# A fused four-layer block on one NeuronCore: layernorms at three stage seams moved off GpSimd and worked by token groups, and maxima added by VectorE in the last softmax

## The reference

```python
x = x + _layernorm(attention(_layernorm(x)))     # 16 heads, band of 64 on either side
x = x + _layernorm(kmoe_ffn(_layernorm(x)))      # top 2 of 64 Kronecker experts
x = x + _layernorm(state_space(_layernorm(x)))
x = x + _layernorm(soft_moe(_layernorm(x)))

def state_space(x):                # inner width 256, state 64
    x_input, x_gate = split(x @ W_in.T)
    u = silu(causal_conv4(x_input) + conv_b)
    Bu = u @ W_B.T
    h_t = 0.95 * h_(t-1) + 0.05 * Bu_t                     # along the tokens
    y = (hs @ W_C.T + D_param * u) * silu(x_gate)
    y = y @ W_out.T
    return _layernorm(y + x) * ln_gamma + ln_beta

def soft_moe(x):                   # 64 experts, 32 slots each
    logits = (x @ phi_w.T + phi_b).reshape(tokens, 64, 32)
    D = softmax(logits, over the slots);  C = softmax(logits, over the experts)
    X = tanh(_layernorm(sums of x over all tokens, weighted by D))   # one row a slot
    return C @ (X @ expert_w + expert_b)
```

## Time and profile before

| | |
|---|---|
| device time, median of 3 runs | 782.77 us (781.86 to 792.21) |
| the profiled execution's own time | 791.13 us |
| its span | 789.4 us |
| TensorE busy | 656.1 us, 83% |
| VectorE busy | 475.5 us, 60% |
| ScalarE busy | 359.4 us, 46% |
| GpSimd busy | 340.2 us, 43% |
| mean granted clock of TensorE | 0.903 |

### The profile page before, as it was taken

One profiled execution on the slowest core, in us unless ns is written; L12 is line 12 of the kernel. 1 busy time (PEld: TensorE's weight loads), 2 busy tenths in 40 slices (PEclk: granted clock), 3 DMA queues, 4 the chain that ended last, 5 costly groups with the idle time before them and its releaser, 6 DMA issues. The chain is left out here.

```text
span 789.4 us, 17996 instructions
## 1 busy us (share of the span) xinstructions
PE 656.1 (83%) x7326; PEld 373.9 (47%) x7326; DVE 475.5 (60%) x1242; ACT 359.4 (46%) x633; POOL 340.2 (43%) x368
## 2 busy tenths in 40 slices
PE   3598989999869999798828860799989879999995
PEld 1314545555427988677724430333333344444442
DVE  6556757785263334261375869699999861424455
ACT  3604646666657335242337431655445454334410
POOL 3004646666520000000015351299989927856531
PEclk9956979999788999898778995799999989999999
DMA  4523240000036400000019000000000000000000
GB/s 87 95 68 47 56 61 10 4 4 4 2 138 199 99 12 4 3 2 4 5 35 360 14 1 0 0 0 1 1 0 0 1 1 1 0 1 13 1 13 27
DMA packets 18389, 27.17 MB, mean 34 GB/s; under 512 B 3699, under 2 KB 16948, under 8 KB 17284
## 3 DMA queue, kind: packets, MB, share of 16 engines
q1 hardware_dynamic: 17390, 25.82, 13.0%
q10 hardware_dynamic: 918, 0.21, 0.2%
HBM read 18.11 MB, written 1.05 MB: 24 GB/s over the span
## 5 line engine op out<-in xcount | busy, mean ns | idle before, releaser
L491 ACT ACTIVATE at_exp<-at_psum 128x512 f32<-128x512 f32 x136 | 78.2, 606 | 62.3 <-PE at_psum L608 59.8
L1592 POOL TENSOR_TENSOR all_phi_b<-all_phi_b,mo_work 128x512 f32<-128x512 f32 x56 | 71.0, 1268 | 44.5 <-ACT mo_work L1798 40.1
L838 POOL TENSOR_TENSOR all_x<-all_x,ff_x_blocks 128x512 f32<-128x512 f32 x3 | 3.9, 1286 | 170.4 <-ACT ff_x_blocks L1029 170.4
L1613 PE MATMUL all_psum<-all_phi,mo_xt 128*128 128x512 f32 x128 | 66.1, 643 | 7.3 <-ACT mo_work L1780 5.6
L306 POOL TENSOR_SCALAR_AFFINE_SELECT at_exp<-at_exp 128x512 f32<-128x512 f32 x68 | 43.1, 634 | 63.9 <-ACT at_exp L491 63.9
L1562 POOL TENSOR_TENSOR mo_work<-mo_work,mo_max 128x1024 f32<-128x1024 f32 x32 | 61.4, 1920 | 21.3 <-DVE mo_max L1854 21.3
L363 DVE TENSOR_REDUCE at_neg_max<-at_psum 128x2 f32<-128x512 f32 x68 | 47.0, 691 | 33.6 <-PE at_psum L595 33.5
L1646 PE MATMUL all_psum<-mo_xt,all_phi_centred 128*128 128x512 f32 x128 | 66.2, 598 | 0.0
L1798 ACT ACTIVATE mo_work<-all_psum 128x512 f32<-128x512 f32 x64 | 37.7, 601 | 61.8 <-PE all_psum L1646 61.8
L595 PE MATMUL at_psum<-at_k_stack,at_q_stack 49*128 49x256 bf16 x272 | 59.1, 306 | 6.2 <-DMA at_k_stack<-at_part_l 3.2
L1699 PE MATMUL all_psum<-mo_work,mo_y_slots 128*128 128x512 f32 x128 | 62.5, 595 | 1.8 <-DVE mo_work L1902 1.8
(11 more groups left out here) (346 smaller groups left out, 1329.6 us busy)
## 6 DMA issues: line engine op xcount, KB each, us to landing
all_expert_w<-in_expert_w SPq DMA_DIRECT2D x1, 4096.0 KB, 18.1
ff_b_up<-in_b_up SPq DMA_DIRECT2D x1, 2048.0 KB, 9.7
ff_a_up<-in_a_up SPq DMA_DIRECT2D x1, 2048.0 KB, 14.1
ff_w_down<-in_w_down SPq DMA_DIRECT2D x2, 1024.0 KB, 18.7
at_q_stack<-at_part_h SPq DMA_DIRECT2D x24, 64.0 KB
at_k_stack<-at_part_h SPq DMA_DIRECT2D x24, 64.0 KB
at_q_stack<-at_part_m SPq DMA_DIRECT2D x16, 64.0 KB
at_k_stack<-at_part_m SPq DMA_DIRECT2D x16, 64.0 KB
```

Source lines behind the costliest of these rows:

```text
L491: nc.scalar.activation(e[:, m // 2, 2 * (m % 2):2 * (m % 2) + 2, :, :].rearrange("p h j q -> p (h j q)"), psum[:, ST + n % 3, :], ACT.Exp, ...
L1592: nc.gpsimd.tensor_tensor(tot[:, ch % 2, :], first, ec[:, ch % 2, j, :], ALU.add).then_inc(added, 1)
L1613: last = nc.tensor.matmul(psum[:, 2 * hf + k, :], xt[:, P * z:P * z + P], phi_d[:, HALF * hf + W * k:HALF * hf + W * k + W], start=True, s ...
```

## The change

1. `Norm.variance` folds the division by 128 into the root (`scale=1/P` in the ScalarE instruction) and has one operation less.
2. At the end of `kmoe` GpSimd adds nothing any more. VectorE adds each group to `x` (`add_x`, 128x512 at once, group 3 in two halves) and at once takes statistics and factors of the next stage's layernorm for groups 0 to 2; VectorE and ScalarE scale two tiles of each. The nine loads of `ssm` are issued in `kmoe`, behind that stage's own.
3. `ssm` starts with the last four tiles only. TensorE transposes quarter 0, runs `project(0)`, transposes quarters 1 to 3, and runs `project(1)`. ScalarE copies quarters 0 and 1, then takes the root of the last group, then `take_x(0)`. `project` waits bank by bank.
4. The bias of `phi` enters PSUM as a second product with one row of 1/128 (`inv_row`), so GpSimd neither scales nor adds it. VectorE gates the last quarter (`gated(3)`).
5. At the end of `ssm` ScalarE scales all tiles of both norms in groups (0 to 11, 12 to 15), VectorE applies gamma and beta as 128x512 products and sums, adds to `x` and takes the statistics of `soft_moe`'s layernorm for tiles 0 to 11; ScalarE scales 8 of them, and TensorE, after 12 products whose result nothing reads, transposes the first quarter. `soft_moe` starts with the last four tiles and the logits.
6. In the combine the 40 blocks from n = 24 on get their maxima from VectorE: the maxima of chunks 1 to 3 are spread once into SBUF (`spread_max`, three products, ScalarE copies them), `combine_logits` loses its first product, VectorE writes logits plus maxima to SBUF (`lower`, `BEHIND` = 2 blocks behind the logits), and ScalarE exponentiates there in place. The bank comes free when VectorE has read it. The inverse of chunk ch+1 is taken at block 13 of chunk ch.

Cut to what is spoken of below:

```diff
-                for gr in range(3):
-                    g.wait_ge(ln_y.by_act, 4 * gr + 4)
-                    nc.gpsimd.tensor_tensor(x[:, 4 * gr:4 * gr + 4, :], x[:, 4 * gr:4 * gr + 4, :], y_rows[:, 4 * gr:4 * gr + 4, :], ALU.add)
...
+                def add_x(gr, step=4):
+                    for t in range(4 * gr, 4 * gr + 4, step):
+                        dve.wait_ge(ln_y.by_act, t + step)
+                        v.tensor_tensor(x[:, t:t + step, :], x[:, t:t + step, :], y_rows[:, t:t + step, :], ALU.add).then_inc(nx["added"], step)
+
+                def next_norm(gr):
+                    add_x(gr)
+                    dve.wait_ge(nx["added"], 4 * gr + 4)
+                    for t in range(4 * gr, 4 * gr + 4):
+                        nx["ln"].tile_stats(t, x[:, t, :])
+                    nx["ln"].variance(dve, 4 * gr, 4 * gr + 4)
+
+                def next_scale(gr):
+                    nx["ln"].invert(dve, 4 * gr, 4 * gr + 4, gr)
+                    for t in range(4 * gr, 4 * gr + 4, 2):
+                        nx["ln"].scale(t, nx["xn"][:, t, :], x[:, t, :]).then_inc(nx["ln"].by_dve, 1)
...
                 take_y(0)
-                for gr in range(4):
-                    norm_y(gr)
-                    if gr < 3:
-                        take_y(gr + 1)
-                    ln_y.invert(dve, 4 * gr, 4 * gr + 4, gr)
-                for t in range(12, NT):
-                    dve.wait_ge(ln_y.by_act, t + 1)
-                    v.tensor_tensor(x[:, t, :], x[:, t, :], y_rows[:, t, :], ALU.add)
+                norm_y(0)
+                take_y(1)
+                invert_y(0)
+                norm_y(1)
+                take_y(2)
+                invert_y(1)
+                next_norm(0)
+                next_scale(0)
+                norm_y(2)
+                take_y(3)
+                invert_y(2)
+                next_norm(1)
+                norm_y(3)
+                next_scale(1)
+                invert_y(3)
+                next_norm(2)
+                add_x(3, 2)
+                next_scale(2)
...
+                transposes(0)
+                pe.wait_ge(loaded, LOADS)
                 project(0)
+                for ch in range(1, NC):
+                    transposes(ch)
                 project(1)
...
-                    nc.tensor.matmul(psum[:, k, :], centre[:, :], s["phi"][:, W * k:W * k + W], start=True, stop=True).then_inc(phi_done, 1)
+                    nc.tensor.matmul(psum[:, k, :], centre[:, :], s["phi"][:, W * k:W * k + W], start=True, stop=False)
+                    nc.tensor.matmul(psum[:, k, :], inv_row[:, :], s["phi_b"][0:1, W * k:W * k + W], start=False, stop=True).then_inc(phi_done, 1)
                 out(NC - 1)
...
+                pe.wait_ge(ln_o.by_act, 4)
+                for _ in range(WARM):
+                    nc.tensor.matmul(psum[:, 0, :].rearrange("p (k n) -> p k n", k=4), c["identb"][:, :], c["identb"][:, :].unsqueeze(1).broadcast_to([P, 4, P]), start=True, stop=True)
+                transposes_next(0)
...
+                take_xt(0)
+                take_xt(1)
+                ln_x.root(act, 12, NT, 3)
...
                 take_x(0)
+                take_xt(2)
+                act.wait_ge(ln_x.factors, 4)
+                for t in (13, 15):
+                    nc.scalar.activation(xn[:, t, :], x[:, t, :], ACT.Identity, bias=ln_x.tmp[:, 1, t:t + 1], scale=ln_x.tmp[:, 6, t:t + 1]).then_inc(ln_x.by_act, 1)
                 take_gate(0)
                 take_x(1)
+                take_xt(3)
...
+                ln_z.root(act, 0, 12, 0)
+                act.wait_ge(ln_z.factors, 1)
+                normed(ln_z, z, z, 0, 12)
+                ln_z.root(act, 12, 16, 1)
+                act.wait_ge(ln_z.factors, 2)
+                normed(ln_z, z, z, 12, 16)
...
-                residual(NC - 2)
-                residual(NC - 1)
-                ln_z.finish(dve)
...
+                residual(2)
+                ln_z.variance(dve, 0, 12)
+                gated(NC - 1)
+                ln_z.invert(dve, 0, 12, 0)
+                residual(3)
+                ln_z.variance(dve, 12, 16)
+                shift(0)
+                ln_z.invert(dve, 12, 16, 1)
+                shift(1)
+                shift(2)
+                och.settle(dve)
+                for q in range(3):
+                    stats_o(q)
+                ln_o.variance(dve, 0, 12)
+                shift(3)
+                ln_o.invert(dve, 0, 12, 0)
+                och.settle(dve)
+                stats_o(3)
+                ln_o.variance(dve, 12, 16)
+                add(0)
+                stats_n(0)
+                ln_o.invert(dve, 12, 16, 1)
+                add(1)
+                stats_n(1)
+                add(2)
+                stats_n(2)
+                ln_n.variance(dve, 0, 12)
+                add(3)
+                ln_n.invert(dve, 0, 12, 0)
...
                     cols = slice(W * ch, W * ch + W)
-                    nc.tensor.matmul(psum[:, n % 3, :], selp[:, :], mp_t[:, cols], start=True, stop=False)
-                    nc.tensor.matmul(psum[:, n % 3, :], phi[:, P * j:P * j + P], xt[:, cols], start=False, stop=True).then_inc(cl_done, 1)
+                    if n not in by_dve:
+                        nc.tensor.matmul(psum[:, n % 3, :], selp[:, :], mp_t[:, cols], start=True, stop=False)
+                    nc.tensor.matmul(psum[:, n % 3, :], phi[:, P * j:P * j + P], xt[:, cols], start=n in by_dve, stop=True).then_inc(cl_done, 1)
...
+                def spread_max(k):
+                    if k == 0:
+                        pe.wait_ge(mp_ready, 2)
+                    else:
+                        pe.wait_ge(spread_ready, k)
+                    nc.tensor.matmul(psum[:, 3, :], selp[:, :], mp_t[:, W * k + W:W * k + 2 * W], start=True, stop=True).then_inc(spread_done, 1)
...
+                        act.wait_ge(lowered, before(n) + 1)
+                        nc.scalar.activation(part, part, ACT.Exp).then_inc(ec_ready, 1)
+                        return
...
+                def lower(n):
+                    ch, j = n // NJ, n % NJ
+                    dve.wait_ge(cl_done, n + 1)
+                    if n == by_dve[0]:
+                        dve.wait_ge(spread_ready, 3)
+                    if ch >= 2:
+                        dve.wait_ge(y_done, n - 2 * NJ + 1)
+                    v.tensor_tensor(ec[:, ch % 2, j, :], psum[:, n % 3, :], max_spread[:, ch - 1, :], ALU.add).then_inc(lowered, 1)
...
+                invert_total(0)
                 for ch in range(NCH):
-                    invert_total(ch)
                     for j in range(NJ):
+                        if j == 13 and ch + 1 < NCH:
+                            invert_total(ch + 1)
                         scale(ch, j)
+                        if NJ * ch + j + LEAD - BEHIND in by_dve:
+                            lower(NJ * ch + j + LEAD - BEHIND)
```

291 lines of the change are left out of this document (169 added, 122 removed).

## The result

The changed kernel takes 788.82 us (median of 20 runs, 774.35 to 795.35). The kernel before, run as often, takes 791.50 (781.86 to 798.33); the 782.77 of its first three runs stood at the low end of that spread. The ratio is 0.9892, with a 95% interval of 0.9857 to 0.9927. A second comparison, with 12 runs of the changed kernel and 19 of the one before, gave 784.24 against 790.51, ratio 0.9953 (0.9907 to 0.9999). The change is worth some 3 to 8 us: 2.7 and 6.3 by the medians, 8.5 and 3.7 by the ratios. That is less than the 2% that the forecast counted as a difference, but more than its "-0.3".

A forecast was written before the change was run, and what follows sets the result against it. No engine was full over the span; the late engine varied by seam and loop, GpSimd pacing dispatch and TensorE the combine. Terms 3.5 + 0.8 - 4.6 = -0.3 gave 782.5 us against 782.77; range 773 to 790, 8 in 10.

The forecast's parts named there:

- -0.3: Whole kernel: the summed change in us, from 3.5 and 0.8 at the seams and -4.6 in the combine.
- Combine, -4.6: Combine: TensorE saves 8.1 us, of which 3.4 turn into a wait for GpSimd, leaving -4.6 us.
- -7.5 if the wait stays 1.44: Combine: the term's fast bound, -7.5 us if the wait before the last sum stays 1.44 us.
- Seam one, +3.5: Expert to state-space stage: ScalarE's second copy waits behind the projection, so the first recurrence starts 3.5 us later.
- The recurrence carries it unchanged: State-space loop: the 3.5 us delay passes through unchanged, as later periods hold the same operations in order.
- Seam two, +0.8: State-space to last stage: GpSimd's unbroken row begins 52.8 us after the last recurrence instead of 51.96, +0.8 us.
- 3.70 becomes 6.9: Seam two: TensorE's centred weights with bias, sixteen halves instead of eight, take 6.9 us instead of 3.70.
- Attention loses one small operation per variance ...: nothing: Attention: the shorter variance saves 0.08 us at four places, counted as nothing.
- level of 782.5: Whole kernel: the forecast time in us, tied to the earlier kernel's median of 782.77.
- forecast's own case of -3 to +2.5: Whole kernel: the forecast's main case, a change of -3 to +2.5 us, chance 0.55.
- first rival's: Both seams pay as the change says: terms +1.4, -2.0, -4.6, giving 777.6 us; chance 0.14.
- the second's: Combine keeps nearly all of its 8.1 us: terms +3.5, +0.8, -7.5, giving 779.6 us; chance 0.15.

The follow-up runs named there:

- e5: Changed kernel with the third chunk's norm behind the last maxima, 22 warming products instead of 12 before the last stage, 7 in the state-space loop: 789.14 us, ratio 0.9988.
- e2: Changed kernel with ScalarE taking the first convolution input before the second copy of the transposed input: 789.30 us, ratio 0.9982 to the kernel before.
- e6: Kernel before with the shorter variance alone, nothing else of the change: 783.81 us against 788.27, ratio 0.9950.
- e10: As e8, with 11 more warming products ahead of the first stage's first scores: 769.33 us, ratio 0.9799 to the kernel before.
- e4: Changed kernel with the last four tiles' root taken before the first logits, their inversion and scaling before the first maxima: 786.49 us, ratio 0.9903 to the kernel before.
- e1: Changed kernel with the combine's maxima added by TensorE again for all 64 blocks: 795.40 us, ratio 1.0085 to the kernel before.
- e8: As e7, but 30 warming products at the expert stage's end, none in the loop, 12 later ones before the last stage: 774.28 us, ratio 0.9833 to the kernel before.
- e7: Changed kernel with all repairs (ScalarE order, later slot weights, root first, late third-chunk norm, 36, 7 and 22 warming products): 775.79 us against 788.27 before.

## Why the prediction was right, and where it was not

- *Combine, -4.6*: measured -4.8 and -4.0 (153.82 and 154.78 against 158.66 and 158.80). Rounds of 1.72, a pass of 0.60, the norm in front of the last four maxima, the last sum at a wait of 4.10: each step as it was put. The bound "-7.5 if the wait stays 1.44" would have needed e5's edit, which gave 2 us and left the wait at 2.02.
- *Seam one, +3.5*: measured +2.9 and +2.2. The mechanism is the one named, ScalarE's second copy behind the projection at half clock; e2 shows it. The term was 0.6 too large against the first pair of profiles, since the transposes came 0.8 before the forecast 414.6.
- *"The recurrence carries it unchanged"*: failed. The loop took 28.65 instead of 26.92, since the clock fell at the second quarter's input product. It is not the seam's doing alone: e6, whose seam and loop are those of before, lost 2.3 us in the loop with the same product at 3.47 us, and e10's loop took 27.00. Such a fall goes with when TensorE's pauses come, which the working left out.
- *Seam two, +0.8*: measured +1.9 and +3.2. The mis-sized term is the centred weights with the bias: "3.70 becomes 6.9" measured 8.43, so the residual came 14.4 us behind the recurrence where the working had 12.8. The first logits came 40.45 behind the recurrence for 39.6 in the working, so nearly all of the 1.0 us by which the first profile's row is late (53.84 for 52.8) stood ahead of the last stage. Behind it the lock of 1.89 us beside GpSimd's first subtraction was named for the expert stage but not looked for here, and 1.1 us could be won there (e4).
- *"Attention loses one small operation per variance ...: nothing"*: this is the step that failed by most, as far as the timed runs tell. With the variance alone the kernel gained 4.5 us, without it the change lost 3.5 to 8.1. The size of the edit said nothing about it.
- The sum of the terms behind the expert stage, -0.3, measured +1.1 to +3.7. With a gain of 2.7 us by the medians and 8.5 by the ratio, the first two stages must have given some 4 to 12 us. The time of 788.82 lies in the range, and "within 2%" came true, but the sum was right partly by luck: what was missed behind the expert stage (+1.4 to +4.0) and what was put at nothing ahead of it have opposite signs. By the medians the -2.7 lies just inside the forecast's own case of -3 to +2.5, by the ratio it lies outside, and either way the gain comes from where the forecast had none. It is not the first rival's (the seams did not pay) nor the second's (the combine did not keep its 8.1). The level of 782.5 missed by 6.3 us, because the median of three runs that it was tied to, 782.77, stood 8.7 below that of twenty.

**Open.** That the variance acts through the first stage's clock is an inference: the timed runs show its gain, the profiles show that the clock there differs from run to run by up to 11 us of that stage, and in e10's profile, with the pause ahead of the first scores filled, the fall is absent. The pause's length alone doesn't decide: e1 waited 1.30 us there and fell, the second profile of the changed kernel waited 1.31 and didn't, after its earlier fall. The one profile of e6 had the half clock at 38 us all the same, and with three profiles of the longer variance against eleven of the shorter, how often the shorter one avoids it stays open. That the loop's fall at the second quarter can be held off by warming wasn't settled either.

## What to carry to other kernels

Before pricing an edit by its instructions, look in the windows of the trace for stretches at half clock and for the pause ahead of each: there a fall of the clock or none was worth eleven microseconds between two executions of one kernel, in a stage that the change hardly touches. Compare two profiles of the same kernel stretch by stretch first; only stretches that repeat can carry a verdict of a microsecond, and a pause of two microseconds that only waits for transfers is worth an attempt to fill it with idle products, right up to the work: a pause left behind them lost the clock again (e8). And when work is taken from in front of an engine, ask what it did for that engine's clock.

## What the runs showed of the hardware

- With a row of 11 idle bfloat16 products of 128x512 in the pause ahead of the first scores (0.47 us of it left), TensorE stayed at 2.4 GHz over the next 26 us (e10). Ten of thirteen profiles without them, with 1.3 to 3.3 us of pause, fell to 1.2; the other three had fallen earlier, at 22 to 24 us, and were back at the high level by 31.
- The clock also fell in the middle of work without a pause: at about 470 us in e5, after more than ten microseconds of products back to back. And a clock that 4.5 us of warming products had brought back to 1.00 for the transposes was at 0.50 again after a pause of 1.86 us (e8).
- One execution (e7) stood at 0.95 in nearly every window. The Trainium skill (TensorE: Matmul & The Clock Gate, The HAM clock gate) calls the rate binary, half or full, with a third state only once three cores of a die are busy; this kernel ran on one core, and the rows of this execution differ.
- A VectorE operation on 128x4 elements lasted 1.89 us when it began beside a GpSimd subtraction of 1.91 us with two SBUF inputs, and 0.16 without (the changed kernel and e4).
